# A group's weighing in two pieces and the next pair's projections at other steps of a hand-ordered attention loop

## What is computed

```python
q, k, v = proj(Wq, bq), proj(Wk, bk), proj(Wv, bv)      # (B, 16, 256, 8) each
scores = einsum('bhqd,bhkd->bhqk', q, k) * sm_scale
o = einsum('bhqk,bhkd->bhqd', softmax(scores), v)
attn = einsum('bse,fe->bsf', o, Wo) + bo

x = x + 0.5 * ffn(layernorm(x))
x = x + attn(layernorm(x))
x = x + 0.5 * ffn(layernorm(x))
```

## Time and profile before

| | us |
|---|---|
| median of 3 runs | 619.1 (618.34 to 622.76) |
| profiled execution, its own time | 617.05 |
| its span | 615.2 |

### The profile page before, as it was taken

How to read it: one execution, slowest core, us unless ns; L and a number is a source line. 1 busy time by engine, 2 the same in 40 slices (tenths; PEclk the granted TensorE clock), 3 DMA queues, 4 the chain that set the end, 5 groups by cost and what they waited for, 6 DMA issues and landing times.

```text
span 615.2 us, 12580 instructions
## 1 busy us (share of the span) xinstructions
PE 589.1 (96%) x4452; PEld 439.3 (71%) x4452; DVE 443.6 (72%) x1000; ACT 466.4 (76%) x796; POOL 98.3 (16%) x262
## 2 busy tenths in 40 slices
PE   2999999999999999999999999999989999999996
PEld 2788788788686766565656565766678878788785
DVE  7995855868558778798988897885665756855742
ACT  4677977968865578788787878877877977968964
POOL 2092020022021103132231302102020020020000
PEclk9999999999999799999999999999999999999999
DMA  8300000000074306171625343400000001000011
GB/s 282 86 2 1 0 2 1 0 0 1 1 273 145 130 2 220 56 255 62 235 89 187 137 139 142 134 2 1 2 1 1 1 1 36 0 26 8 1 34 37
DMA packets 36693, 42.02 MB, mean 68 GB/s; under 512 B 2464, under 2 KB 27296, under 8 KB 36640
## 3 DMA queue, kind: packets, MB, share of 16 engines
q1 hardware_dynamic: 36640, 41.31, 19.8%
HBM read 22.42 MB, written 18.87 MB: 67 GB/s over the span
## 4 chain that ended last, share of the span: by engine, by line
PE 73%; ACT 9%; DVE 8%; issue 5%; DMA 3%; SPq 1%; POOL 0%; ACTq 0%; DVEq 0%; POOLq 0%
PE bank L1092 39%; PE bank L1204 9%; PE bank L1179 8%; PE bank L1191 4%; PE bank L1193 3%; DVE silu L842 3%; DVE act_lo L833 2%; ACT silu L544 2%; DVE neg_max L883 2%; PE bank L1161 1%; PE bank L1222 1%; PE bank L1169 1%; ACT act_hi L536 1%; ACT act_hi L559 1%; DMA QK<-qk_scratch 1%
## 5 line engine op out<-in xcount | busy, mean ns | idle before, releaser
L1092 PE MATMUL bank<-act_hi,WH 128*128 128x512 f32 x576 | 230.5, 400 | 3.8 <-ACT act_hi L559 1.5
L1092 PE MATMUL bank<-act_lo,WH 128*128 128x512 f32 x576 | 225.7, 392 | 0.0
L883 DVE TENSOR_REDUCE neg_max<-bank 128x2 f32<-128x512 f32 x256 | 166.8, 681 | 32.6 <-PE bank L1179 30.4
L678 ACT ACTIVATE probs<-bank 128x512 f32<-128x512 f32 x256 | 139.3, 598 | 38.6 <-PE bank L1193 37.0
L853 DVE TENSOR_TENSOR act_lo<-full,act_hi 128x512 fp32r<-128x512 f32 x128 | 91.5, 719 | 101.7 <-ACT act_hi L559 101.4
L557 ACT ACTIVATE full<-bank,SG 128x512 f32<-128x512 f32 x128 | 88.1, 688 | 65.8 <-PE bank L1092 65.0
L1092 PEld LDWEIGHTS bank<-act_hi,WH 128*128 128x128 f32 x576 | 108.2, 188 | 31.2 <-ACT act_hi L559 4.7
L1092 PEld LDWEIGHTS bank<-act_lo,WH 128*128 128x128 f32 x576 | 108.3, 188 | 23.1 <-issue 1.0
L1191 PE MATMUL bank<-QK 32*128 32x256 f32 x512 | 96.1, 334 | 0.4 <-ACT probs L678 0.4
L559 ACT ACTIVATE act_hi<-bank,SG 128x512 fp32r<-128x512 f32 x128 | 87.1, 681 | 0.0
L1193 PE MATMUL bank<-m_parts,SEL 32*128 32x256 f32 x512 | 82.1, 280 | 0.0
(11 more groups left out here) (94 smaller groups left out, 570.7 us busy)
## 6 DMA issues: line engine op xcount, KB each, us to landing
qk_scratch<-qk SPq DMA_DIRECT2D x64, 256.0 KB, 2.6
QK<-qk_scratch SPq DMA_DIRECT2D x16, 1024.0 KB, 7.6
raw_rest<-w_ffn SPq DMA_DIRECT2D x4, 512.0 KB, 5.8
out<-X SPq DMA_DIRECT2D x4, 512.0 KB, 3.2
X<-x SPq DMA_DIRECT2D x3, 512.0 KB, 7.7
raw<-w_ffn SPq DMA_DIRECT2D x3, 256.0 KB, 4.5
X<-x SPq DMA_DIRECT2D x2, 256.0 KB, 3.2
WA<-w_att SPq DMA_DIRECT2D x1, 256.0 KB, 5.6
```

Of the source, the lines that this page charges most:

```text
L678: A.activation(probs[:, v % 8, :], bank[B_BANKS[bb][v]][:, :], ACT.Exp, scale=SCALE)\
L883: D.tensor_reduce(neg_max[:, bb, qt, n0:n0 + 2], bank[(banks or A_BANKS[bb])[u]][:, :].rearrange("p (h k) -> p h k", h=2), axis=AX.X, op=A ...
L1092: ins = MM(dst, a, b, start=k == 0, stop=k == len(todo) - 1)
```

## The change

A group's weighing is cut in its two halves in four of the eight gaps of a pair. In the even slot the half `kt = 0` moves from after step 3 to after step 1 and from after step 11 to after step 9; in the odd slot from 3 to 1 and from 7 to 5. The other half stays. In the even slot the tokens of the output move from after step 13 to after step 9 (DVE's part with them, to steps 10 and 11), `project_v` moves from after step 9 to after step 11 (except in the first slot) and waits for `o_norm`, and `transpose_att` of pair i + 2 comes in after step 13. In the odd slot `project_q` moves from 9 to 7 and `project_k` from 11 to 9, and the tokens stay after step 13. DVE's sides follow: the pieces of the normalised x stand at steps 7, 8, 9 and 12 of the even slot, and of the six pieces of the statistics in the odd slot the second to fifth move from steps 5, 7, 8 and 9 to 7, 8, 9 and 10.

```diff
-TOKENS = 13
+TOKENS = (9, 13)
+EARLY_HALF = ((1, 9), (1, 5))
...
@@ ACT, attend
-                    if u == (9 if prev else 5) and v_pair is not None:
+                    if u == (11 if prev else 5) and v_pair is not None:
                         set_v(*v_pair)
-                    if u == 7 and ahead is not None:
+                    if u == 13 and bb == 0 and ahead is not None:
                         x_to_sbuf(ahead)
-                    if u in (9, 11) and ahead is not None:
-                        full_part(ahead, (u - 9) // 2)
-                    if u in (10, 12) and ahead is not None:
-                        high_part(ahead, (u - 10) // 2)
+                    if u in (7, 9) and bb == 1 and ahead is not None:
+                        full_part(ahead, (u - 7) // 2)
+                    if u in (8, 10) and bb == 1 and ahead is not None:
+                        high_part(ahead, (u - 8) // 2)
...
@@ DVE, att_body
-                            for t, u in enumerate((8, 9, 10, 11))}
+                            for t, u in enumerate((7, 8, 9, 12))}
...
-                    odd = dict(zip((4, 5, 7, 8, 9, 11), norm_steps(norm_of(q), 4 * q, 4, halves=True)))
+                    odd = dict(zip((4, 7, 8, 9, 10, 11), norm_steps(norm_of(q), 4 * q, 4, halves=True)))
...
@@ PE, attend
                 def rows_of_max():
-                    if prev2:
+                    if bb == 1 and pair + 2 < NPAIR:
+                        pe.wait_ge(a_xT_sb, pair + 3)
+                    elif bb == 1 and pair + 1 < NPAIR:
+                        pe.wait_ge(v_set, pair + 2)
+                    else:
                         pe.wait_ge(o_norm, b - 1)
-                    elif prev:
-                        pe.wait_ge(v_set, pair + 2)
                     max_rows(b, bb)
...
+                        if v >= 5 and v % 4 == 1 and u in EARLY_HALF[bb]:
+                            weigh(*at, v // 4 - 1, 0)
                         if v >= 7 and v % 4 == 3:
-                            weigh(*at, v // 4 - 1, 0)
+                            if u - 2 not in EARLY_HALF[bb]:
+                                weigh(*at, v // 4 - 1, 0)
                             weigh(*at, v // 4 - 1, 1)
...
+                    if u == (11 if prev else 5) and v_pair is not None:
+
+                        if prev:
+                            pe.wait_ge(o_norm, b)
+                        pe.wait_ge(m_lo, b + 1)
                         project_v(v_pair, 6)
-                    if u == 7 and ahead is not None:
-                        if prev2:
-                            pe.wait_ge(att_added, b - 1)
-                        pe.wait_ge(m_lo, b + 1)
+                    if u == 13 and bb == 0 and ahead is not None:
                         pe.wait_ge(v_set, pair + 2)
                         transpose_att(ahead, 0, 6)
```

More of the change, by code:

```diff
@@ L719, in att_body @@
             def att_body(i, par, ahead=True, more=True, first=False):
-                attend(2 * i, 0, prev=not first, prev2=not first, v_pair=(i + 1, 1 - par) if more else None)
+                attend(2 * i, 0, prev=not first, prev2=not first, v_pair=(i + 1, 1 - par) if more else None,
+                       ahead=i + 2 if ahead else None)
                 attend(2 * i + 1, 1, prev2=not first, ahead=i + 2 if ahead else None)
@@ L1043, in attend @@
                         side[u]()
-                    if u == TOKENS + 1 and prev:
+                    if u == TOKENS[bb] + 1 and prev:
                         norm_o(b - 1)
-                    if u == TOKENS + 2 and prev:
+                    if u == TOKENS[bb] + 2 and prev:
                         scale_o(b - 1)
@@ L1388, in attend @@
                         transpose_x(XN1 + 1, 1, 5)
-                    if u == (9 if prev else 5) and v_pair is not None:
+                    if u == 7 and bb == 1 and ahead is not None:
                         if prev2:
@@ L1393, in attend @@
                         pe.wait_ge(m_lo, b + 1)
+                        project_q(ahead, 6)
+                    if u == 9 and bb == 1 and ahead is not None:
+                        pe.wait_ge(q_full, ahead)
+                        project_k(ahead, 6)
+                    if u == TOKENS[bb] and own and prev:
+                        if bb == 1 and ahead is not None:
+                            pe.wait_ge(k_full, ahead)
+                        else:
+                            pe.wait_ge(att_added, b - 1)
+                        tokens_of_o(b - 1)
+                    if u == (11 if prev else 5) and v_pair is not None:
+                        if prev:
+                            pe.wait_ge(o_norm, b)
+                        pe.wait_ge(m_lo, b + 1)
                         project_v(v_pair, 6)
-                    if u == 7 and ahead is not None:
-                        if prev2:
-                            pe.wait_ge(att_added, b - 1)
-                        pe.wait_ge(m_lo, b + 1)
+                    if u == 13 and bb == 0 and ahead is not None:
                         pe.wait_ge(v_set, pair + 2)
                         transpose_att(ahead, 0, 6)
-                    if u == 9 and ahead is not None:
-                        project_q(ahead, 6)
-                    if u == 11 and ahead is not None:
-                        pe.wait_ge(q_full, ahead)
-                        project_k(ahead, 6)
-                    if u == TOKENS and own and prev:
-                        if ahead is not None:
-                            pe.wait_ge(k_full, ahead)
-                        elif v_pair is not None:
-                            pe.wait_ge(v_set, v_pair + 1)
-                        elif prev2:
-                            pe.wait_ge(att_added, b - 1)
-                        tokens_of_o(b - 1)
             def att_body(i, par, ahead=True, more=True, first=False):
-                attend(2 * i, i, par, 0, prev=not first, prev2=not first, v_pair=i + 1 if more else None)
+                attend(2 * i, i, par, 0, prev=not first, prev2=not first, v_pair=i + 1 if more else None,
+                       ahead=i + 2 if ahead else None)
                 attend(2 * i + 1, i, par, 1, prev2=not first, more=more, ahead=i + 2 if ahead else None)
```

## The result

The changed kernel is slower: a median of 642.71 us (641.75 to 648.55, five runs) against 619.1, a ratio of 1.039 with a 95% interval of 1.032 to 1.046. The time lies in the predicted range (622 to 645), some 9 us above the predicted 633.5 and above the 627 to 640 that the prediction gave its own case. The profiled execution took 641.75 against 617.05.

What follows compares the result with a forecast made beforehand. PE was taken to bound the kernel, busy 28.37 of a middle pair's 28.80 us. Five middle pairs at +2.4 and the edge pairs made +14.5 on 617.05, 631.6; expected median 633.5, range 622 to 645.

Steps and rivals of the forecast that it cites:

- its own case: Whole kernel: the order's waits make it slower, median 633.5 us, own range 627 to 640; chance 0.77.
- Front: Steps 0 to 3 of each slot: stall of 0.41 becomes a 0.37 wait for m_lo, plus the cut; +0.10 us.
- A half costs 0.57: Half a weighing on PE: 0.43 of products plus 0.14 of switching, 0.57 us; bounds 0.50 and 0.65.
- V behind o_norm: Even slot, before v: PE waits 1.17 us for DVE's scaling, seen 2.43 after the tokens; bounds 1.0 and 1.3.
- X behind its last piece: Even slot, after step 13: PE waits 0.86 us for x's last piece, behind the max unit of step 12 on DVE.
- Even slot: Sum of its front, copy wait, cut, two waits and x's work, less the stall in steps 14 and 15: +2.8 us.
- Odd slot: Sum of its front, cut, stall gone, x moved out, and q, k and tokens waits: -0.34, said as -0.4 us.
- At the edges: Pair 6: +2.1 even, +0.3 odd; pair 7: +0.4 and +0.2; pair 0: -0.5; pair 5 counted as a middle pair, +2.4.
- The rival of the smoothing: The waits of v and x don't come, middle pairs gain 0.7 to 1.3 each: 610 to 614 us; chance 0.05.
- the first fall of the clock: Upper end of the range, 645 us; the clock rival gave 642 to 660 for two to six falls.
- the third rival: Even slots: PE idling 2.0 us within 5 halves the clock, some 5 us per fall, 642 to 660; chance 0.10.

Runs made afterwards that it cites:

- The run with m_lo early: On top of the run with early statistics: top_max after ACT's step 0 exponential, split_max behind the max unit of step 1; 621.85 us, ratio 1.003.
- Scaling first: Changed kernel with DVE's reciprocal and scaling of the even slot's tokens ahead of the max unit of step 10; 633.41 us, ratio 1.022.
- The earlier piece: Changed kernel with the pieces of the normalised x at steps 6, 7, 8, 9 instead of 7, 8, 9, 12; 637.01 us, ratio 1.029.
- the run with the waits filled: Changed kernel with idle 128x512 products in its two waits, four before v and three before x; 639.68 us, ratio 1.031.
- the run with early statistics: Changed kernel with x's pieces at steps 6 to 9, tokens scaled before step 10's max unit, odd-slot statistics at steps 3 to 8; 625.5 us, ratio 1.010.
- the run of the moves alone: Changed kernel with no early half (EARLY_HALF empty), moved transposes and projections kept; 637.12 to 649.61 us, ratio 1.032.
- the split alone: Kernel before with nothing but the four early halves of the weighings; 631.45 us, ratio 1.019.

## Why the prediction was right, and where it was short

The mechanism was right at each step of the sum, and the sizes were close.

- *Front.* Predicted +0.10, the stall turned into a wait. Steps 2 and 3 went from 1.11 to 0.69, and transpose_o starts 0.36 behind the half's end (321.68 against 320.75 + 0.57), predicted 0.37. The run with m_lo early took it away at 0.34 to 0.36 a slot.
- *A half costs 0.57.* Measured 0.57 (309.90 to 310.47). The Trainium skill (TensorEngine Tiling (Array Packing), Key Properties) says that a change of the tiling mode drains the engine. The trace agrees in so far as a half of two rounds of 0.215 leaves 0.14; no row shows the drain itself.
- *V behind o_norm.* Predicted 1.17, measured 1.16 from the half's end (313.47 less 312.31), of which 1.09 is shown as idle, six times. Scaling first took 1.15 a slot away.
- *X behind its last piece.* Predicted 0.86, measured 0.86, five times. The earlier piece took 0.71 away, v_set kept the rest.
- *Even slot.* Predicted +2.8, measured +2.9. *Odd slot.* Predicted -0.4, measured -0.47 where POOL doesn't disturb it (slots 7 and 9); whether it does was luck within hundredths of a microsecond. The pair came to 31.23, predicted 31.2.
- *At the edges* the sum was a little low: pair 5's odd slot gained 0.06 (read from the run with the waits filled) where 0.4 were taken, pair 6 cost 2.9 (predicted 2.4) and pair 7 1.0 (predicted 0.6).
- *The rival of the smoothing* is out in this form. Its core, that a more even front is worth 0.27 a slot, is right only once the chain to m_lo is shortened too.

The predicted median was 9 us too low, for two reasons, and the time is in the stated range only because that reached up to the first fall of the clock.

The first is a sentence on the odd slot: "The order on POOL and SP is unchanged and q and k come earlier, so the writes and loads of QK gain room." It looked only at what the earlier q and k free, and not at what POOL's two subtractions of 1.28 now run beside. They came to lie over DVE's small operations. In slots 1, 3 and 5 that is 0.83, 0.98 (with the 0.5 of the clock taken off) and 0.92, by the difference to the run with early statistics: 2.7 us. In the terms of the sum: what POOL does to DVE stood in it at nothing, and was 2.7. The GPSIMD Engine Reference of the Trainium skill (Key points) says that GpSimd shares its SBUF interfaces with VectorE, with contention for VectorE instructions in a 2-port perf mode or with two SBUF inputs. The rows go with the contention (in them it is one-input TENSOR_SCALARs that are long), but none of them shows a mode or which of an instruction's ports was held.

The second is the third rival. It had a chance of 0.10 and a place in the range, and it came true in part: two falls in the profile, in slots 2 and 10, worth 5.7 us against the run with the waits filled. It priced a fall at some 5 us, for a whole slot; these lasted 6.8 us and cost 2.9 each, and the two of 17.1 in the run of the moves alone 6.0 each. So the sum for slots 1 to 14 is 23.4 = 5.7 clock + 2.7 POOL + 15.0 for the order itself, predicted 14.5 for all sixteen slots. The bound that I took against it, 1.52 of idle at full clock between dense products, was from the feed-forward part; in the attention the clock fell behind two waits of 1.1 and 0.9 within 4 us in some slots and not in others. That the two together were needed is likely and not shown: the middle pairs with one of them (two profiles) or with none kept the clock, but at the end of the attention it fell behind one wait of 1.05 in two profiles, not in others with the same wait, and behind 0.25 in one.

In the medians the same two terms are an account, not a measurement: where the clock fell in the unprofiled runs isn't recorded, only their mean clock. That mean does say that there were more falls than the one at the start: 0.983, in the run at the median, is 22 us at half rate, where the longest fall at the start in any profile was 17 and the one at the end of the changed kernel's profile takes 2 of its span. With the waits filled it was 0.988 or 0.989 in all four runs, which is the profile's own fall at the start and no more.

## What to carry to other kernels

When a stage is moved past others on one engine, count the distance from each producer to its consumer in the other engine's own queue: o_norm was due 2.4 us after the tokens by the order on DVE (2.7 with DVE's backlog in the run of the moves alone), and two steps and a half of a weighing, 1.26 us, don't cover that. A stall taken away uncovers the next chain (here m_lo, 0.04 shorter than the stall), so shorten that one with it, or nothing moves. And look at what a moved operation of another engine will newly run beside, and at short idle of PE close together: here they cost 8.4 us on top of the 15.0 of the order itself.

## What the runs showed of the hardware

- A DVE tensor_scalar on 128x4 values takes 0.16 us alone. Where it started 0.05 to 1.1 us into a tensor_tensor of POOL in SBUF (128x512, 1.28 us, or 128x256, 0.72) it ended within 0.03 of POOL's end in every case in the attention of every profile here, and so took 0.28 to 1.29. Within the first 0.05 it went either way: 1.25 to 1.30, or its own 0.16, and then POOL's took 1.34 to 1.38 (ten cases). In the last 0.06 it lost nothing. It happened in the changed kernel and, by moving the statistics alone, in the kernel before. Max reductions out of PSUM that started under the same POOL instructions took 0.69 at most, as elsewhere.
- Behind waits of PE of 1.1 and 0.9 us within 4 us the granted clock fell to 0.50 twice in one execution and not in its other three middle pairs, and twice in that of the moves alone; with either wait alone (profiles of one execution each) it didn't fall in slots 2 to 11, and with both waits kept but filled by products nobody reads it didn't either. A fall in a middle pair lasted 7 us in after and 17 in the run of the moves alone. At the end of the attention it also fell behind one wait of 1.05 (3.4 us, the split alone and the earlier piece of x) and with 0.25 of idle in 8 us (10 us, m_lo early), so this account of the falls is not whole.
- The same fall at the start of the attention is in every profile without the idle products and lasts from 3.4 to 17 us over the profiles of this study. With 1.6 us of idle products in that place the mean clock was 0.998 to 1.000 in fourteen of fourteen runs, the kernel 5 us faster and the spread of its runs 3 us instead of 7.
- Up to the first max_rows all kernels run the same program, and it took 203.08 us in one profile and 206.49 in another. A difference of 3 us between single profiles is therefore no finding here; slots are compared instead.
